# Exponentials over two PSUM banks at once in a cross-attention and mixture-of-experts kernel

## The reference, cut to what matters

```
x = x + attention(layernorm(x), ctx, ctx, mask)     # 8 sequences of 512, 16 heads of 32
    sim  = (q @ k^T) * 32**-0.5, masked, softmax over keys
    out  = (softmax(sim) @ v) @ Wo + bo
x = x + moe(layernorm(x))                           # 8 experts, top 512 tokens each
```

## Time and profile before

| | us |
|---|---|
| median of three runs | 1743.27 (1743.13 to 1743.9) |
| the profiled execution, its own time | 1742.76 |
| its span | 1741.0 |
| PE, ACT and DVE busy in the span | 1618.4, 984.0 and 1112.2 |

### The profile page before, as it was taken

The page is one execution under the profiler, slowest core; times in us unless marked ns, Lnnn a source line. Parts: engine busy times, 40 slices in busy tenths (PEclk is TensorE's granted clock), DMA queues, the critical chain, the costliest instruction groups (busy, mean ns, idle before and its releaser), DMA issues.

```text
span 1741.0 us, 22258 instructions
## 1 busy us (share of the span) xinstructions
PE 1618.4 (93%) x7831; PEld 1162.9 (67%) x7831; DVE 1112.2 (64%) x1950; ACT 984.0 (57%) x2115; POOL 292.7 (17%) x381
## 2 busy tenths in 40 slices
PE   5799989899898998998988699999999999999997
PEld 4556656466465665664744478788888888888885
DVE  6676776867858768578674567766454545454543
ACT  3798788897988878879876222223232323232321
POOL 3121130311211303113012110102020202020100
PEclk9889999999999999999999899999999999999998
DMA  6453543643627435345270142334333333434340
GB/s 205 129 163 94 172 133 97 194 136 122 183 62 213 120 118 171 110 150 155 80 232 31 61 134 97 104 122 129 120 112 130 100 134 102 145 93 156 95 123 25
DMA packets 132712, 219.90 MB, mean 126 GB/s; under 512 B 17276, under 2 KB 51216, under 8 KB 132600
## 3 DMA queue, kind: packets, MB, share of 16 engines
q1 hardware_dynamic: 115960, 175.85, 32.2%
q0 software_dynamic: 16640, 42.61, 9.0%
HBM read 159.02 MB, written 58.87 MB: 125 GB/s over the span
## 4 chain that ended last, share of the span: by engine, by line
PE 78%; DVE 9%; ACT 7%; DMA 3%; issue 2%; SPq 0%; POOL 0%; DVEq 0%; POOLq 0%
PE ps_gen L716 8%; PE ps_gen L718 8%; PE ps_gen L717 8%; PE ps_gen L1829 7%; PE ps_gen L1831 7%; PE ps_gen L1830 7%; PE ps_att L1676 6%; PE ps_gen L1665 5%; PE ps_gen L1643 5%; ACT ps_gen L1070 3%; PE ps_gen L1629 3%; PE ps_gen L1630 3%; PE ps_gen L1631 3%; ACT p_ring L1082 2%; PE ps_gen L1692 2%
## 5 line engine op out<-in xcount | busy, mean ns | idle before, releaser
L1256 DVE TENSOR_REDUCE nmax<-ps_gen 128x1 f32<-128x512 f32 x512 | 337.9, 683 | 128.5 <-PE ps_gen L1643 128.0
L1070 ACT ACTIVATE ps_gen<-ps_gen,nmax 128x512 f32<-128x512 f32 x512 | 343.6, 676 | 59.7 <-DVE nmax L1256 59.7
L1082 ACT ACTIVATE p_ring<-ps_gen,keep_scale 128x512 f32<-128x512 f32 x512 | 336.8, 696 | 64.1 <-PE ps_gen L1665 64.1
L1139 ACT ACTIVATE gel<-ps_gen,b_cols 128x512 f32<-128x512 f32 x128 | 88.3, 690 | 448.9 <-PE ps_gen L718 448.8
L1511 DVE TENSOR_TENSOR gel_lo<-gel,gel_hi 128x512 fp32r<-128x512 f32 x126 | 87.2, 692 | 281.6 <-ACT gel_hi L1140 281.6
L1643 PE MATMUL ps_gen<-kst,qst 97*128 97x512 f32 x512 | 207.0, 427 | 14.2 <-ACT ps_gen L1070 11.5
L1665 PE MATMUL ps_gen<-qst,kst 99*128 99x512 f32 x512 | 196.6, 435 | 24.2 <-ACT ps_gen L1070 15.0
L716 PE MATMUL ps_gen<-hT_hi,w_hi 128*128 128x512 f32 x512 | 202.2, 395 | 0.2 <-DVE hT_lo L1504 0.2
L718 PE MATMUL ps_gen<-hT_hi,w_lo 128*128 128x512 f32 x512 | 199.5, 390 | 0.0
L717 PE MATMUL ps_gen<-hT_lo,w_hi 128*128 128x512 f32 x512 | 199.4, 389 | 0.0
L1829 PE MATMUL ps_gen<-w_hi,gel_hi 128*128 128x512 f32 x504 | 198.1, 393 | 0.0
(11 more groups left out here) (204 smaller groups left out, 2668.9 us busy)
## 6 DMA issues: line engine op xcount, KB each, us to landing
w_raw<-in_L_ffn_W SPq DMA_DIRECT2D x128, 512.0 KB, 5.0
kst<-qk_rows SPq DMA_DIRECT2D x96, 256.0 KB, 3.9
qst<-qk_rows SPq DMA_DIRECT2D x96, 256.0 KB, 4.8
x_in<-in_x POOLq DMA_DIRECT2D x60, 256.0 KB, 3.5
qk_rows<-kT_hi SPq DMA_DIRECT2D x32, 256.0 KB, 2.0
qk_rows<-kT_lo SPq DMA_DIRECT2D x32, 256.0 KB, 2.0
qk_rows<-qT_hi SPq DMA_DIRECT2D x32, 256.0 KB, 2.0
qk_rows<-qT_lo SPq DMA_DIRECT2D x32, 256.0 KB, 3.6
```

Source lines behind the costliest of these rows:

```text
L1070: e.activation(psum[:, :], psum[:, :], ACT.Exp, bias=nmax[g % 2][:, c], scale=-1.0, accum_out=den[g % 2][:, c]).then_inc(drained_sem("max" ...
L1082: e.activation(p_ring[n % NP_][:, :], ps("score", g, kt, h)[:, :], ACT.Exp, scale=keep_scale[:, b:b + 1]).then_inc(drained_sem("score", g, ...
L1256: e.tensor_reduce(nmax[g % 2][:, h * TB + t:h * TB + t + 1], ps("max", g, h, t)[:, :], AX.X, ALU.min).then_inc(s_min, 1)
```

## The change

Scores are taken in pairs. `take_pair` picks two neighbouring banks of one double tile (`ps_pair`, 2 x 512 columns; three of them, and `ps_one`, which other steps alone can take), the pair whose later-used bank is the least recent among the pairs with no open bank. The scores of heads 0 and 1 stand next to each other as before, and those of heads 2 and 3 now do too. ACT runs one exponential of 128x1024 for both, waiting for both banks, and it writes one of three tiles of twice the width. Each bank now keeps a count of drains apart from its count of uses, since one exponential drains two banks. The tables of places and the lags are set anew.

```diff
+    def take_pair(self, key, other):
+
+        pairs = [(k, k + 1) for k in range(0, NGEN - 1, 2) if not {k, k + 1} & self.bank_open]
+        i, j = min(pairs, key=lambda p: max(self.bank_order.index(k) for k in p))
+        self.use_bank(key, i)
+        self.use_bank(other, j, key)
+
+    def scores(self, g, kt, h):
+        self.take_pair(("score", g, kt, h), ("score", g, kt, h + 1))
+        self.add("score", g, kt, h)
+        self.add("score", g, kt, h + 1)
...
-    LOAD_C_AT, SPLIT_C_AT = (-0.26, 0.33), (0.29, 0.48)
-    LOAD_X_AT, STATS_X_AT = (0.28, 0.41), (0.66, 0.95)
...
+    LOAD_C_AT, SPLIT_C_AT = (-0.35, 0.23), (0.09, 0.48)
+    LOAD_X_AT, STATS_X_AT = (0.20, 0.31), (0.67, 0.95)
...
-            a.with_bank("score", i, kt, 0)
-            a.with_bank("score", i, kt, 1)
+            a.scores(i, kt, 0)
             fill(time[0])
             if before[0] >= 0:
                 attend(*before)
             fill(time[1])
-            a.with_bank("score", i, kt, 2)
+            a.scores(i, kt, 2)
             fill(time[2])
-            a.with_bank("score", i, kt, 3)
             fill(time[3])
             fill(time[4])
...
-        ps_gen = [top.enter_context(nc.psum_tensor(f"ps_gen{i}", [P, BANK], F32)) for i in range(NGEN)]
+        ps_pair = [top.enter_context(nc.psum_tensor(f"ps_pair{i}", [P, 2 * BANK], F32)) for i in range(NGEN // 2)]
+        ps_one = top.enter_context(nc.psum_tensor("ps_one", [P, BANK], F32))
+        ps_gen = [pair[:, k * BANK:(k + 1) * BANK] for pair in ps_pair for k in range(2)] + [ps_one[:, :]]
...
-        p_ring = [sb(p1, f"p_ring{i}", [P, S]) for i in range(NP_)]
+        p_pair = [sb(p1, f"p_pair{i}", [P, 2 * S]) for i in range(NP_ // 2)]
+        p_ring = [pair[:, k * S:(k + 1) * S] for pair in p_pair for k in range(2)]
...
-                elif kind == "score":
+                elif kind == "score" and at[2] % 2:
                     g, kt, h = at
                     b = g // GB
-                    n = (g * KT + kt) * HG + h
+                    n = (g * KT + kt) * HG + h - 1
                     on.wait_ge(*drained("scale"))
                     on.wait_ge(s_w_lo, W_NO["o"])
+                    on.wait_ge(*full("score", g, kt, h - 1))
                     on.wait_ge(*full("score", g, kt, h))
                     if n >= NP_:
-                        on.wait_ge(s_av, (n - NP_) // HG + 1)
-                    e.activation(p_ring[n % NP_][:, :], ps("score", g, kt, h)[:, :], ACT.Exp,
-                                 scale=keep_scale[:, b:b + 1]).then_inc(drained_sem("score", g, kt, h), 1)
+                        on.wait_ge(s_av, (n + 1 - NP_) // HG + 1)
+                    e.activation(p_pair[n // 2 % (NP_ // 2)][:, :], ps_pair[agenda.bank["score", g, kt, h - 1][0] // 2][:, :], ACT.Exp,
+                                 scale=keep_scale[:, b:b + 1]).then_inc(drained_sem("score", g, kt, h - 1), 1)
```

More of the change, by code:

```diff
@@ L71, in __init__ @@
         self.bank_order = list(range(NGEN))
+        self.bank_drains = [0] * NGEN
+        self.bank_last = [None] * NGEN
+        self.drain = {}
+        self.before = {}
         self.bank_open = set()
@@ L113, in take_bank, with use_bank @@
     def take_bank(self, key):
-        i = next(k for k in self.bank_order if k not in self.bank_open)
+        self.use_bank(key, next(k for k in self.bank_order if k not in self.bank_open))
+        return self.bank[key][0]
+    def use_bank(self, key, i, drained_with=None):
         self.bank_order.remove(i)
@@ L120, in take_bank @@
         self.bank_uses[i] += 1
-        return i
+        self.before[key] = self.bank_last[i]
+        self.bank_last[i] = key
+        if drained_with is None:
+            self.bank_drains[i] += 1
+            self.drain[key] = (i, self.bank_drains[i])
+        else:
+            self.drain[key] = self.drain[drained_with]
+    def take_pair(self, key, other):
[7 more added lines that the diff above has]
+        self.add("score", g, kt, h + 1)
     def put_late(self, key, step):
@@ L301, in attention_agenda @@
[L301 to L307, removed]
+        "sync": {"mask_row": 0.08, "keep_hi": -0.05, "keep_lo": 0.00, "stack_hi": 0.12, "stack_lo": 0.16, "out": 0.03, "x1_norm": 0.13, "back": 0.57},
@@ L599, in drained, with all_drained @@
         def drained(*key):
-            i, use = agenda.bank[key]
-            return s_drained[i], use + 1
+            i, count = agenda.drain[key]
+            return s_drained[i], count
         def free(*key):
-            i, use = agenda.bank[key]
-            return s_drained[i], use
+            before = agenda.before[key]
+            return drained(*before) if before else (s_drained[0], 0)
+        def all_drained(i):
+            return drained(*agenda.bank_last[i])
         def full_sem(*key):
@@ L610, in drained_sem @@
         def drained_sem(*key):
-            return s_drained[agenda.bank[key][0]]
+            return s_drained[agenda.drain[key][0]]
         W_NO = {"k": 0, "q": 4, "v": 8, "o": 12}
```

32 lines of the change are left out of this document (19 added, 13 removed).

## The result

Over 14 runs each, side by side on the same chips, the changed kernel takes 1750.3 us (1746.57 to 1755.89) against 1741.3 (1735.79 to 1743.9): **1.0063 of the time before, interval 1.0052 to 1.0074**. It is slower, where 0.7% faster was forecast. The ratios aren't those of the medians, which are 9.0 us apart in both sets. So the loss is 7 to 11 us, and two sets of the same program can differ by a quarter of a per cent, 4 us; smaller differences between two experiments are treated as none.

A forecast was written before the change was run, and what follows sets the result against it. PE, busy 93% of the span, was taken as the bound, with ACT setting the pace in two stretches a sequence. Terms 10.2 + 2.5 + 2.3 - 3.2 = 11.8 us off the 1743.27 median gave 1731 us, range 1712 to 1750.

The forecast's parts named there:

- All the rest: Terms beside the wide exponential: context splits 2.5 us, loads of x 2.3, scores together -3.2, banks and remaining places 0.
- The wide exponential's own price: On ACT in attention: one 128x1024 exponential holds ACT 0.99 us against 1.14 for two, saving 0.15 us a pair.
- Banks, "I charge 0": PSUM banks of score pairs: held 0.65 us longer, charged 0, from 26 us lost to nothing gained.
- The third rival: Banks run out: PE stops at scores, 0.65 us at each of 40 places, at most 26 us, time 1757; chance 18%.
- The rival's sign: What would show banks running out: PE waiting for line 1113 at many scores.
- The 10.2 us for the pairs: Two stretches where ACT is full: 8.5 pairs a sequence at 0.15 us, eight sequences, 10.2 us gained (0 to 15.0).
- The scores together: Scores of heads 2 and 3 adjacent on PE: 0.23 us more before transposed maxima, 14 places, 3.2 us lost.
- The splits and the loads of x: Next sequence's context splits moved earlier fill ACT's idle 0.35 us, 2.5 us gained; x landing earlier spares DVE waits, 2.3.
- The remaining places, priced "at nothing": Other table entries shift work by a few hundredths of a 28.5 us group; same work, no PE gap there, 0 us.
- The first rival: PE's gaps close and the clock stays up: half of some 21 us comes back, time 1721; chance 20%.
- The second rival: Nothing moves: ACT's idle time swallows the saving, pairs bring about 0, time 1742 (1740 to 1746); chance 15%.

The follow-up runs named there:

- both sets: The changed kernel, unedited, run in two sets against the kernel before: 1.0063 in the first, 1.0038 in the second.
- pair_banks_single_exp: Changed kernel with its pairs of banks and new places, but one 128x512 exponential per score, each draining its own bank; 1.0039 of the kernel before.

## Why the prediction was wrong

The time was forecast at 1731 us and came out at 1750.3, 19 us above. The experiments on the new places divide this in two. The wide exponential was to bring 10.2 us and brought nothing or cost 4 (`pair_banks_single_exp` against the two sets of the changed kernel). All the rest was to bring 1.6 us and costs 7, since the kernel without the wide exponential is at 1.0039.

**The wide exponential's own price** was right: 0.99 us of ACT forecast, 1.01 us read; 1.12 us long forecast, 1.115 measured. ACT was to be busy for 7 to 8 us less in a sequence, and it is for 5.4: that sign took 696 ns twice, without the overlap that a pair of exponentials already had in the rows, and busy time doesn't count the overlap twice.

**Banks, "I charge 0",** is the step that failed. It set the second score's 0.23 us and the longer hold against gaps on PE that I took for cover. What was not in the sum at all is the wait of the first exponential for the second score, with everything behind it on ACT. On the old places that wait costs 12 us and the common release about 5, together 17 (1.0065 to 1.0165), against the 10 that one instruction gives. The third rival named the hold and priced it at up to 26 us; it had 18% and should have had more. The measured 1750.3 lies three quarters of the way from my forecast to its 1757, and just above the range. The range's 1750 takes in three quarters of that rival's price, and not half of it as the text says. The rival's sign, PE waiting for line 1113 at many scores, came (20 times, 7.6 us), but at a third of the size that 26 us asks for.

**The 10.2 us for the pairs** was 8.5 pairs a sequence in two stretches where ACT is full. Between two kernels that both wait for both scores one instruction came out at 10 us, which agrees in number and not in mechanism: PE's idle time didn't shrink, from 79.1 to 79.8 us, and the granted clock of the runs rose from 0.964 to 0.970. I call the agreement luck. In the kernel before, the same ACT time is worth 4 us (2 to 7), so the term was too large by more than twice. A full ACT isn't a bound by itself: my windows showed ACT's busy time alone, and DVE's beside it would have shown 7.20 of 8 us in a stretch of that kind.

**The scores together**, 3.2 us by count of one score at 14 places, measured 9 us on the old places and nothing or a gain on the new ones. PE's idle time grew by 3 us on the old places. The other 6 us are time in which PE works; the granted clock of the runs, 0.9685 against 0.9701, is an estimated 3 us of them at most, and the rest stays open.

**The splits and the loads of x** were to bring 4.8 us. The loads did land early: DVE's waits for them went from 2.5 us to 0.5 in the changed profile. The maxima were copied later all the same, so this gain didn't reach the end of the group. It wasn't tried alone.

**The remaining places, priced "at nothing"**, were wrong by the most: the tables are worth 7 to 12 us to the pairs and cost the kernel before 17. Among them was a step past a queue that I had in the order and didn't read: POOL's first context load had moved ahead of the third tile's `rstd`, 2 to 4 us in one sequence.

**The first rival**, the clock coming back, didn't come. The two profiles have 0.974 and 0.972, but over all runs the changed kernel was granted 0.969 in both sets, and the kernel before 0.971 beside the second. **The second rival**, "nothing moves", fits the steady part of the profile: sequences of 114.1 us, PE idle for 38 us of 22 groups in both kernels, and ACT's idle time grown. Its 1740 to 1746 us misses what the order, the banks and the places cost.

## What to carry to other kernels

Merging two instructions into one merges their waits and their releases; cost both before the fixed overhead is booked as a gain, because together they can be larger (here 17 us against 10). An engine that is full in a stretch need not be its bound: shorten it alone, with everything else held, and see what comes back (here 4 of 34 us) before trading anything for it. An order fitted to one rotation of buffers has to be fitted again for another, and one step moved in it can cost 10 us, so a mechanism has to be judged with its own fitted order beside its own opposite. And compare the granted clock over all runs, not in one profile: here PE's idle time explained 3 us of a step of 12.

## What the runs showed of the hardware

An activation that reads two neighbouring PSUM banks runs at the rate of one: 1115 ns for 1024 columns against 696 for 512, 0.82 ns for each further column, the same as copies from SBUF in the earlier trace rows.
